# Loading two pairs of the last round in four pieces of 16, 49, 49 and 14 partitions

## The chip, the cores and the metric

The kernel runs on one core of a Trainium2 chip. The metric is the device time of one execution in microseconds, the median over runs.

## What is computed

```python
def reference(x, itok_B_1_198, itok_B_0_7, fside_8xS_0, L0_cond_weights, L1_cond_weights):
    # x (128, 128, 1024) f32; weights (200, 128, 128) and (8, 128, 128); bias (8, 128)
    x = x + einsum('bct,bcd->bdt', x, L0_cond_weights[itok_B_1_198])
    x = x + einsum('bct,bcd->bdt', x, L1_cond_weights[itok_B_0_7]) + fside_8xS_0[itok_B_0_7][:, :, None]
    return x
```

Each of the 128 batches has a matrix x of 128 channels by 1024 steps. It goes through two residual layers, each with a weight chosen by the batch's own index out of a table of 200 or 8. Input and output are 67.1 MB each.

## The kernel before

The two layers are folded into one matrix. With J = I + W1 (the identity plus the chosen second weight) a batch's result is (W0 J + J) applied to x, plus the bias. TensorE makes the product W0 J (`product`, L237, into `m_ps`), VectorE adds J (`sum_m`, L318, into `m_sb`), TensorE applies the sum to x (`results`, L254, into `y_ps`), and the bias is added on the way out of PSUM: the left half of 512 steps by VectorE (`left`, L326), the right half by ScalarE (`right`, L350). Both write back into the buffer from which x was read.

Work goes in pairs of batches. A pair's x is one row of 8 KB in each of 128 partitions, 1 MB. The buffer `xy` is a ring of 8 slots, one pair each; 64 pairs make 8 rounds of 8 slots. The host lays x and out in memory as pairs, so that a load or a store of a pair is one DMA of 128 rows.

The order of the work is written out by hand, engine by engine:

- SyncE's queue issues all loads. For each slot it issues first the two weights W0 of the pair two slots ahead (`load_w0`, L108 to L128, 64 KB each; a weight that an earlier batch has already brought is skipped through the DMA's condition, L113), then waits until the slot's store of the round before has landed (L159), then issues the load of x (`load_x`, L131). The rounds 1 to 6 are a loop (L149), the last round is written out (L156 to L160). The very last pair, slot 7 of the last round, is loaded in four quarters of 512 steps (L165), and two of its four quarters of the result are stored from this queue (L171).
- GpSimd copies each batch's weight and J to the places at which TensorE reads them (`pick`, L188 and L190).
- TensorE runs, for each slot, the first batch of the slot before, the product of this slot, and the second batch of the slot before. It waits for a slot's load (L246), for its summed matrix (L247), and for the PSUM banks to be emptied (L253). Rounds 1 to 7 are one loop (L274), and the last pair stands behind it (L283).
- ScalarE, besides the right halves, issues each pair's store (`store`, L359), and the other two quarters of the last pair (L376).

A DMA adds 16 to its semaphore in all when everything that it moves has landed; a wait for 16 more therefore means that the whole pair is there. Each slot has its own semaphore for loads (`x_loaded[s]`) and for stores (`stored[s]`).

Of the kernel before, what the change touches and what calls it, by code (L numbers as in the profile page):

```python
# [1 line left out]

# [9 lines left out]
def conditioned_residual_kernel(nc, x, cond, w0_t, w1_bias, out):  # L12
# [11 lines left out]
    NP, C, KP, T = x.shape  # L24
    B = NP * KP
    N0, _, D = w0_t.shape
    N1 = w1_bias.shape[1]
    assert C == D == 128
    PAIR = KP
    RING = 8  # L30
    PAIRS = B // PAIR
    ROUNDS = PAIRS // RING
    LAST = RING - 1
# [2 lines left out]
    HALF = T // 2  # L36
    MB = 2
    YB = 2
    assert PAIRS % RING == 0 and HALF <= 512 and RING % MB == 0 and ROUND_B % YB == 0

    x_v = x.rearrange("n c k t -> n c (k t)")
    out_v = out.rearrange("n c k t -> n c (k t)")

    with ExitStack() as ctx:
        def sb(name, shape, dt=F32):
            return ctx.enter_context(nc.sbuf_tensor(name, shape, dt))

        def sem(name):
            return ctx.enter_context(nc.semaphore(name))


        xy = sb("xy", [C, RING, PAIR, T])
# [17 lines left out]
        home_less_b = sb("home_less_b", [B, 1])  # L70
        y_ps = ctx.enter_context(nc.psum_tensor("y_ps", [D, YB, 2, HALF], F32))
        m_ps = ctx.enter_context(nc.psum_tensor("m_ps", [C, MB, 512], F32))
# [12 lines left out]
        x_loaded = [sem(f"x_loaded{s}") for s in range(RING)]  # L85
        w0_loaded = [sem(f"w0_loaded{s}") for s in range(RING)]
        stored = [sem(f"stored{s}") for s in range(RING)]
        last_x_loaded = [sem(f"last_x_loaded{n}") for n in range(2 * PAIR)]
        last_stored = sem("last_stored")
        eye_cleared = sem("eye_cleared")  # L90
# [5 lines left out]
        y_ready = sem("y_ready")  # L96
        left_out = [sem(f"left_out{s}") for s in range(YB)]
        right_out = [sem(f"right_out{s}") for s in range(YB)]

        def half(h):  # L100
            return slice(h * HALF, (h + 1) * HALF)
# [3 lines left out]
        @block.sync  # L105
        def _(sp):
            def words_of(words):
                return nc.values_load_multi_w_load_instructions(  # L108
                    words, engines=(mybir.EngineType.SP,),
                    skip_runtime_bounds_check_because="each word is checked against its own range below")[1]  # L110

            def load_one(b, s, i, needed):
                sp.dma_start(w0_home[:, bass.ds(b, 1), :].rearrange("k b c -> k (b c)"),  # L113
                             w0_t[bass.ds(nc.s_assert_within(i, 0, N0 - 1), 1), :, :].rearrange("n k c -> (n k) c"),  # L114
                             cond=needed).then_inc(w0_loaded[s], 16)

            def load_w0_first(s):
                words = words_of(cond_words[0:1, 0, s * PAIR:(s + 1) * PAIR])
                for k in range(PAIR):
                    load_one(s * PAIR + k, s, words[k], None)  # L120

            def load_w0(r, s):

                sp.wait_ge(w0_loaded[s], r * (PAIR * 16))  # L124
                b = r * ROUND_B + s * PAIR
                words = words_of(load_words[0:1, bass.ds(b, PAIR), :].rearrange("o b f -> o (b f)"))
                for k in range(PAIR):
                    load_one(b + k, s, words[2 * k], nc.s_assert_within(words[2 * k + 1], 0, 1))  # L128

            def load_x(r, s):  # L130
                sp.dma_start(xy[:, s, :, :].rearrange("c k t -> c (k t)"),  # L131
                             x_v[bass.ds(r * RING + s, 1), :, :].rearrange("n c f -> (n c) f"))\
                  .then_inc(x_loaded[s], 16)


            sp.dma_start(j_all[:].rearrange("c n d -> c (n d)"), w1_bias.rearrange("c n d -> c (n d)"))\
              .then_inc(w1_loaded, 16)
            load_x(0, 0)
            sp.wait_ge(cond_loaded, 16)
            for s in range(RING):  # L140
                load_w0_first(s)
                if s < LAST:
                    load_x(0, s + 1)


            sp.wait_ge(home_ready, 4)
            for s in range(LEAD):
                load_w0(1, s)
            with sp.Fori(1, ROUNDS - 1) as r:  # L149
                for s in range(RING):  # L150
                    load_w0(*((r, s + LEAD) if s + LEAD < RING else (r + 1, s + LEAD - RING)))

                    sp.wait_ge(stored[s], r * 16)
                    load_x(r, s)

            for s in range(RING - 1):  # L156
                if s + LEAD < RING:
                    load_w0(ROUNDS - 1, s + LEAD)
                sp.wait_ge(stored[s], (ROUNDS - 1) * 16)  # L159
                load_x(ROUNDS - 1, s)  # L160

            sp.wait_ge(stored[LAST], (ROUNDS - 1) * 16)
            for k in range(PAIR):
                for h in range(2):
                    sp.dma_start(xy[:, LAST, k, half(h)], x[NP - 1, :, k, half(h)])\  # L165
                      .then_inc(last_x_loaded[2 * k + h], 16)
            for k in range(PAIR):

                b = LAST * PAIR + k
                sp.wait_ge(left_out[b % YB], (ROUNDS - 1) * (ROUND_B // YB) + b // YB + 1)  # L170
                sp.dma_start(out[NP - 1, :, k, half(0)], xy[:, LAST, k, half(0)]).then_inc(last_stored, 16)  # L171

            sp.wait_ge(last_stored, 2 * PAIR * 16)
# [51 lines left out]
        @block.tensor  # L225
        def _(pe):
            def product(r, s, first=False):

                pe.wait_ge(picked, r * RING + (s + 1))
                if first:  # L230
                    pe.wait_ge(w0_loaded[s], PAIR * 16)
                if not first or s >= MB:

                    pe.wait_ge(m_ready[s % MB], r * (RING // MB) + s // MB)
                for k in range(PAIR):
                    w0_of_k = w0_home[:, s * PAIR + k, :] if first else w0_pick[:, s, k, :]
                    last = nc.tensor.matmul(m_ps[:, s % MB, k * D:(k + 1) * D], w0_of_k,  # L237
                                            j_pick[:, s, k, 0:D], start=True, stop=True)
                last.then_inc(product_ready, 1)

            def results(r, s, k, first=False, last=False):

                b = s * PAIR + k
                if k == 0:
                    if not last:
                        pe.wait_ge(x_loaded[s], r * 16 + 16)  # L246
                    pe.wait_ge(m_ready[s % MB], r * (RING // MB) + (s // MB + 1))  # L247
                for h in range(2):
                    if last:
                        pe.wait_ge(last_x_loaded[2 * k + h], 16)  # L250
                    if not first or b >= YB:

                        pe.wait_ge((left_out, right_out)[h][b % YB], r * (ROUND_B // YB) + b // YB)  # L253
                    nc.tensor.matmul(y_ps[:, b % YB, h, :], m_sb[:, s, k, :], xy[:, s, k, half(h)],  # L254
                                     start=True, stop=True).then_inc(y_ready, 1)


            pe.wait_ge(ones_ready, 1)
            pe.wait_ge(cond0_row_ready, 1)
            nc.tensor.matmul(cond0_ps[:, 0:B], ones[:], cond0_row[:], start=True, stop=True)  # L260
            nc.tensor.matmul(cond0_ps[:, B:B + 1], cond0_row[:], ones[0:1, 0:1], start=True, stop=True)\  # L261
              .then_inc(cond0_spread, 1)


            product(0, 0, first=True)
            pe.wait_ge(eye_ready, 1)
            pe.wait_ge(home_step, 4)
            nc.tensor.matmul(home_ps[0:1, 0:B], home_less_b[:], eye[:], start=True, stop=True)\  # L268
              .then_inc(home_turned, 1)
            for s in range(1, RING):  # L270
                results(0, s - 1, 0, first=True)
                product(0, s, first=True)
                results(0, s - 1, 1, first=True)
            with pe.Fori(1, ROUNDS) as r:  # L274
                results(r - 1, LAST, 0)
                product(r, 0)
                results(r - 1, LAST, 1)
                for s in range(1, RING):
                    results(r, s - 1, 0)
                    product(r, s)  # L280
                    results(r, s - 1, 1)
            for k in range(PAIR):
                results(ROUNDS - 1, LAST, k, last=True)  # L283

# [120 lines left out]
```

## Time and profile before

| | us |
|---|---|
| median of 3 runs | 352.03 |
| lowest and highest | 350.3 and 352.62 |
| the profiled execution | 353.64 |
| its span in the profile | 351.9 |
| busy in it: TensorE / VectorE / ScalarE / GpSimd | 281.1 / 126.3 / 97.0 / 65.3 |
| moved by DMA | 140.80 MB, mean 400 GB/s |
| granted TensorE clock, mean | 0.93 |

The span is what the profile's rows cover, from the first to the last instruction; the device time lies 1.7 us above it. PE is TensorE, PEld its weight loads, DVE VectorE, ACT ScalarE, POOL GpSimd, SP SyncE; a q behind a name is the engine's own queue of DMA and register instructions. A DMA share of 1.00 means that sixteen DMA engines are busy; where two queues' packets overlap on one engine it goes a little over 1.

### The profile page before, as it was taken

The numbers are of one execution on the slowest core, as the hardware profiler recorded it, in microseconds if no ns is written. First come the engines' busy times: TensorE is split into PE (matmuls) and PEld (weight loads), VectorE is DVE, ScalarE is ACT, GpSimd is POOL, SyncE is SP. The second block draws the span as 40 slices with busy tenths as digits, with TensorE's granted clock in tenths as the row PEclk, the third lists the DMA queues.
The fourth block names the chain that finished last, engine by engine and source line by source line (L and its number), as shares of the span: only waits on it lengthen the run. The fifth ranks groups of instructions, "written<-read, shape, count | busy, mean of one in ns | idle before, by whom it ended". The sixth has DMA issues, their size and how long they took to land.

```text
span 351.9 us, 5351 instructions
## 1 busy us (share of the span) xinstructions
PE 281.1 (80%) x774; PEld 135.6 (39%) x774; DVE 126.3 (36%) x202; ACT 97.0 (28%) x135; POOL 65.3 (19%) x249
## 2 busy tenths in 40 slices
PE   2898499859959977985985996998399678686894
PEld 2454245324424533532532533443155233342341
DVE  3354134404423522441541541444035334342441
ACT  1133035302413321520341331443034212232232
POOL 2400041113113112212212212330131121221200
PEclk9999789969978988998998996999789999999998
DMA  7999999999999999999999999999999999999966
GB/s 282 372 414 422 410 401 413 405 407 403 427 423 424 417 399 419 408 420 386 377 424 415 422 425 422 424 424 420 424 390 401 425 422 415 424 377 415 401 261 247
DMA packets 32554, 140.80 MB, mean 400 GB/s; under 512 B 3617, under 2 KB 15266, under 8 KB 16418
## 3 DMA queue, kind: packets, MB, share of 16 engines
q1 hardware_dynamic: 23184, 74.14, 53.7%
q10 hardware_dynamic: 9362, 66.59, 45.2%
q14 instruction: 7, 0.06, 0.0%
q8 instruction: 1, 0.02, 0.0%
HBM read 76.03 MB, written 67.11 MB: 407 GB/s over the span
## 4 chain that ended last, share of the span: by engine, by line
SPq 44%; DMA 36%; issue 9%; PE 8%; ACT 1%; ACTq 0%
DMA xy<-x 27%; SPq L113 16%; SPq L131 13%; DMA out<-xy 8%; SPq L108 8%; PE y_ps L254 8%; SPq L114 4%; SPq L128 3%; PE m_ps L237 1%; ACT xy L350 1%; DMA cond_words<-cond 0%; SPq L149 0%; ACTq L359 0%; SPq L124 0%; ACTq L358 0%
## 5 line engine op out<-in xcount | busy, mean ns | idle before, releaser
L254 PE MATMUL y_ps<-xy,m_sb 128*128 128x512 f32 x512 | 257.2, 640 | 53.1 <-DMA xy<-x 52.0
L254 PEld LDWEIGHTS y_ps<-xy,m_sb 128*128 128x128 f32 x512 | 96.6, 204 | 162.4 <-issue 130.9
L350 ACT ACTIVATE xy<-y_ps,j_pick 128x512 f32<-128x512 f32 x128 | 88.0, 687 | 236.7 <-PE y_ps L254 236.5
L326 DVE TENSOR_SCALAR xy<-y_ps,j_pick 128x512 f32<-128x512 f32 x128 | 96.1, 751 | 156.3 <-PE y_ps L254 156.3
L188 POOL COPY w_pick<-w_home 128x128 f32 x112 | 32.9, 293 | 258.2 <-issue 258.2
L237 PEld LDWEIGHTS m_ps<-j_pick,w_pick 128*128 128x128 f32 x224 | 37.3, 209 | 30.9 <-issue 30.5
L318 DVE TENSOR_TENSOR m_sb<-m_ps,j_pick 128x256 f32<-128x256 f32 x64 | 27.2, 424 | 57.4 <-PE m_ps L237 54.5
L237 PE MATMUL m_ps<-j_pick,w_pick 128*128 128x128 f32 x224 | 37.0, 291 | 0.0
L190 POOL COPY j_pick<-j_all 128x129 f32 x112 | 33.0, 295 | 0.1
L237 PE MATMUL m_ps<-j_pick,w_home 128*128 128x128 f32 x32 | 6.5, 338 | 10.0 <-issue 6.0
L350 ACT ACT_TABLE_LOAD x7 | 9.0, 1283 | 13.7 <-POOL j_pick L202 7.4
L237 PEld LDWEIGHTS m_ps<-j_pick,w_home 128*128 128x128 f32 x32 | 6.0, 242 | 14.3 <-issue 9.6
L202 POOL COPY j_pick<-j_all 128x129 f32 x16 | 4.7, 295 | 9.9 <-issue 9.5
L260 PE MATMUL cond_ps<-cond_row,ones 1*128 1x128 f32 x2 | 0.8, 482 | 2.4 <-DVE cond_row L289 2.4
L292 DVE TENSOR_TENSOR j_all<-j_all,eye 128x1024 f32<-128x1024 f32 x1 | 1.2, 1225 | 1.9 <-DMA j_all<-w_bias 1.9
L260 PEld LDWEIGHTS cond_ps<-cond_row,ones 1*128 1x128 f32 x2 | 0.5, 306 | 2.4 <-issue 2.4
L309 DVE TENSOR_TENSOR load_words<-home_ps,batch_less_b 1x128 int32<-1x128 f32 x1 | 0.3, 280 | 2.4 <-PE home_ps L268 2.4
L289 DVE CAST cond_row<-cond_words 1x128 f32<-1x128 int32 x1 | 0.2, 215 | 2.1 <-DMA cond_words<-cond 2.1
L268 PE MATMUL home_ps<-eye,home_less_b 128*1 128x128 f32 x2 | 0.6, 394 | 0.0
L261 PEld LDWEIGHTS cond_ps<-ones,cond_row 1*128 1x128 f32 x2 | 0.5, 328 | 0.0
L261 PE MATMUL cond_ps<-ones,cond_row 1*128 1x1 f32 x2 | 0.4, 277 | 0.0
L299 DVE TENSOR_SCALAR same<-cond_ps,cond_col 128x128 f32<-128x128 f32 x1 | 0.4, 351 | 0.0
(16 smaller groups left out, 2.8 us busy)
## 6 DMA issues: line engine op xcount, KB each, us to landing
xy<-x SPq DMA_DIRECT2D x63, 1024.0 KB, 22.0
out<-xy ACTq DMA_DIRECT2D x63, 1024.0 KB, 9.2
w_home<-w_t SPq DMA_DIRECT2D x128, 64.0 KB
xy<-x SPq DMA_DIRECT2D x4, 256.0 KB, 22.8
j_all<-w_bias SPq DMA_DIRECT2D x1, 516.0 KB, 3.4
out<-xy SPq DMA_DIRECT2D x2, 256.0 KB, 4.4
out<-xy ACTq DMA_DIRECT2D x2, 256.0 KB, 4.1
cond_words<-cond ACTq DMA_DIRECT2D x1, 1.0 KB
```

The costliest lines, as they stand in the source:

```text
L108: return nc.values_load_multi_w_load_instructions(words, engines=(mybir.EngineType.SP,), skip_runtime_bounds_check_because="each word is c ...
L113: sp.dma_start(w0_home[:, bass.ds(b, 1), :].rearrange("k b c -> k (b c)"), w0_t[bass.ds(nc.s_assert_within(i, 0, N0 - 1), 1), :, :].rearra ...
L114: w0_t[bass.ds(nc.s_assert_within(i, 0, N0 - 1), 1), :, :].rearrange("n k c -> (n k) c"),
L128: load_one(b + k, s, words[2 * k], nc.s_assert_within(words[2 * k + 1], 0, 1))
L131: sp.dma_start(xy[:, s, :, :].rearrange("c k t -> c (k t)"), x_v[bass.ds(r * RING + s, 1), :, :].rearrange("n c f -> (n c) f"))\
L188: nc.gpsimd.tensor_copy(w0_pick[:, s, k, :], w0_home[:, bass.ds(home, 1), :].rearrange("k b c -> k (b c)"))
L190: last = nc.gpsimd.tensor_copy(j_pick[:, s, k, :], j_all[:, bass.ds(i, 1), :].rearrange("c n d -> c (n d)"))
L237: last = nc.tensor.matmul(m_ps[:, s % MB, k * D:(k + 1) * D], w0_of_k, j_pick[:, s, k, 0:D], start=True, stop=True)
L254: nc.tensor.matmul(y_ps[:, b % YB, h, :], m_sb[:, s, k, :], xy[:, s, k, half(h)], start=True, stop=True).then_inc(y_ready, 1)
L318: nc.vector.tensor_tensor(m_sb[:, s, :, :], m_ps[:, s % MB, 0:PAIR * D].rearrange("c (k d) -> c k d", k=PAIR), j_pick[:, s, :, 0:D], ALU.a ...
L326: nc.vector.tensor_scalar(xy[:, s, k, half(0)], y_ps[:, b % YB, 0, :], j_pick[:, s, k, D:D + 1], None, ALU.add).then_inc(left_out[b % YB], 1)
L350: nc.scalar.activation(xy[:, s, k, half(1)], y_ps[:, b % YB, 1, :], ACT.Identity, bias=j_pick[:, s, k, D:D + 1]).then_inc(right_out[b % YB ...
```

## The change

In the last round the loads of slots 0 and 3 (`FEWER`) are each issued as four DMAs, for partitions 0 to 15, 16 to 64, 65 to 113 and 114 to 127 (`PIECES`), with a semaphore for each of the two slots that gets 16 from every piece. TensorE's loop ends one round earlier and its last round is written out, since in that round slots 0 and 3 wait for 64 on the new semaphore. All other DMAs, the other waits and the arithmetic stay.

```diff
--- before.py
+++ after.py
@@ -1,3 +1,4 @@
+import itertools
 from contextlib import ExitStack
 
 import concourse.bass as bass
@@ -36,6 +37,8 @@
     HALF = T // 2
     MB = 2
     YB = 2
+    FEWER = (0, 3)
+    PIECES = (0, 16, 65, 114, C)
     assert PAIRS % RING == 0 and HALF <= 512 and RING % MB == 0 and ROUND_B % YB == 0
 
     x_v = x.rearrange("n c k t -> n c (k t)")
@@ -85,6 +88,7 @@
         x_loaded = [sem(f"x_loaded{s}") for s in range(RING)]
         w0_loaded = [sem(f"w0_loaded{s}") for s in range(RING)]
         stored = [sem(f"stored{s}") for s in range(RING)]
+        fewer_loaded = [sem(f"fewer_loaded{s}") for s in FEWER]
         last_x_loaded = [sem(f"last_x_loaded{n}") for n in range(2 * PAIR)]
         last_stored = sem("last_stored")
         eye_cleared = sem("eye_cleared")
@@ -157,7 +161,13 @@
                 if s + LEAD < RING:
                     load_w0(ROUNDS - 1, s + LEAD)
                 sp.wait_ge(stored[s], (ROUNDS - 1) * 16)
-                load_x(ROUNDS - 1, s)
+                if s in FEWER:
+                    for a, b in itertools.pairwise(PIECES):
+                        sp.dma_start(xy[a:b, s, :, :].rearrange("c k t -> c (k t)"),
+                                     x_v[(ROUNDS - 1) * RING + s, a:b, :])\
+                          .then_inc(fewer_loaded[FEWER.index(s)], 16)
+                else:
+                    load_x(ROUNDS - 1, s)
 
             sp.wait_ge(stored[LAST], (ROUNDS - 1) * 16)
             for k in range(PAIR):
@@ -238,11 +248,13 @@
                                             j_pick[:, s, k, 0:D], start=True, stop=True)
                 last.then_inc(product_ready, 1)
 
-            def results(r, s, k, first=False, last=False):
+            def results(r, s, k, first=False, last=False, fewer=False):
 
                 b = s * PAIR + k
                 if k == 0:
-                    if not last:
+                    if fewer:
+                        pe.wait_ge(fewer_loaded[FEWER.index(s)], (len(PIECES) - 1) * 16)
+                    elif not last:
                         pe.wait_ge(x_loaded[s], r * 16 + 16)
                     pe.wait_ge(m_ready[s % MB], r * (RING // MB) + (s // MB + 1))
                 for h in range(2):
@@ -271,7 +283,7 @@
                 results(0, s - 1, 0, first=True)
                 product(0, s, first=True)
                 results(0, s - 1, 1, first=True)
-            with pe.Fori(1, ROUNDS) as r:
+            with pe.Fori(1, ROUNDS - 1) as r:
                 results(r - 1, LAST, 0)
                 product(r, 0)
                 results(r - 1, LAST, 1)
@@ -279,6 +291,13 @@
                     results(r, s - 1, 0)
                     product(r, s)
                     results(r, s - 1, 1)
+            results(ROUNDS - 2, LAST, 0)
+            product(ROUNDS - 1, 0)
+            results(ROUNDS - 2, LAST, 1)
+            for s in range(1, RING):
+                results(ROUNDS - 1, s - 1, 0, fewer=s - 1 in FEWER)
+                product(ROUNDS - 1, s)
+                results(ROUNDS - 1, s - 1, 1)
             for k in range(PAIR):
                 results(ROUNDS - 1, LAST, k, last=True)
```

On SyncE's queue, before, in the last round from slot 0 to slot 1 (`w_home<-w_t` is a weight W0, `xy<-x` a load of x with its partitions by elements):

```order
L131 DMA xy<-x 128x2048 [waits stored0]
L108 TENSOR_LOAD load_words [waits w0_loaded3]
L128 ISA x2
L114 ISA x2
L113 ISA
L113 DMA w_home<-w_t 128x128
```

And in the changed kernel at the same place:

```order
L166 DMA xy<-x 16x2048 [waits stored0]
L166 DMA xy<-x 49x2048 x2
L166 DMA xy<-x 14x2048
L112 TENSOR_LOAD load_words [waits w0_loaded3]
L132 ISA x2
L118 ISA x2
L117 ISA
L117 DMA w_home<-w_t 128x128
```

One DMA of 128 rows has become four, ahead of the weights for slot 3; only the first waits for the slot's store. Slot 3 changes in the same way.

On TensorE, in the changed kernel, behind the loop's branch (`m_ps` is a product, `y_ps` a result; the waits of the first slots of the last round):

```order
L286 COMPARE_AND_BRANCH
L266 MATMUL y_ps<-xy,m_sb 128x512 [waits left_out0,m_ready1,x_loaded7]
L266 MATMUL y_ps<-xy,m_sb 128x512 [waits right_out0]
L247 MATMUL m_ps<-j_pick,w_pick 128x128 [waits m_ready0,picked]
L247 MATMUL m_ps<-j_pick,w_pick 128x128
L266 MATMUL y_ps<-xy,m_sb 128x512 [waits left_out1]
L266 MATMUL y_ps<-xy,m_sb 128x512 [waits right_out1]
L266 MATMUL y_ps<-xy,m_sb 128x512 [waits left_out0,m_ready0,fewer_loaded0]
```

Before, behind the branch, only the last pair stood:

```order
L274 COMPARE_AND_BRANCH
L254 MATMUL y_ps<-xy,m_sb 128x512 [waits left_out0,last_x_loaded0,m_ready1]
L254 MATMUL y_ps<-xy,m_sb 128x512 [waits right_out0,last_x_loaded1]
L254 MATMUL y_ps<-xy,m_sb 128x512 [waits left_out1,last_x_loaded2]
L254 MATMUL y_ps<-xy,m_sb 128x512 [waits right_out1,last_x_loaded3]
```

The matmuls of the last round and their order are the same as in the loop; slots 0 and 3 wait for `fewer_loaded0` and `fewer_loaded3` in place of `x_loaded0` and `x_loaded3`.

## Rows read from the trace of the kernel before

**Rows 1.** The page: DMA busy in tenths over 40 slices, and the stores' queue (packets, MB, share of 16 engines).
```profile
DMA  7999999999999999999999999999999999999966
...
q10 hardware_dynamic: 9362, 66.59, 45.2%
```

**Rows 2.** The chain of waits, its end: start us, us, what.
```profile
310.62 3.55 SPq L131
...
314.22 24.60 DMA xy<-x
...
339.05 1.96 PE y_ps L254 x4
...
341.45 5.24 PE y_ps L254 x12
...
346.71 0.69 ACT xy L350
```

**Rows 3.** Windows near the end: from:to, length, busy time by engine, clock, DMA share, GB/s.
```profile
core 0: us, PE busy (x) PEld busy (x) DVE busy (x) ACT busy (x) POOL busy (x), PEclk, DMA share, GB/s
308.00:333.00 25.00, 18.98 (x58) 9.17 (x59) 8.67 (x14) 6.85 (x10) 4.25 (x16) 1.00 1.01 403
333.00:333.50 0.50, 0.50 (x3) 0.26 (x2) 0.21 (x1) 0.02 (x1) 0.38 (x2) 1.00 1.02 430
333.50:334.00 0.50, 0.50 (x3) 0.07 (x1) 0.42 (x1) 0.00 (x0) 0.32 (x2) 1.00 0.47 197
335.00:336.00 1.00, 1.00 (x4) 0.43 (x3) 0.28 (x1) 0.12 (x1) 0.00 (x0) 1.00 0.08 33
343.50:344.50 1.00, 1.00 (x4) 0.50 (x3) 0.44 (x1) 0.39 (x1) 0.00 (x0) 1.00 0.05 20
```

**Rows 4.** Line L131 (loads) from 282 us on: issues, time to landing.
```profile
L131 SPq DMA_DIRECT2D xy<-x x7: 353/703/3552, 282.9 to 314.2; - x7
...
DMA to landing us min/median/max: 23.5/25.7/27.6
```

**Rows 5.** Line L359 (stores) from 282 us on: issues, time to landing.
```profile
L359 ACTq DMA_DIRECT2D out<-xy x12: 338/339/368, 288.2 to 344.0; - x12
...
DMA to landing us min/median/max: 5.0/8.9/10.4
```

**Rows 6.** Waits of TensorE from 308 us on: total us, times, longest.
```profile
PE y_ps L254 <- DMA xy<-x: 6.5, 6, 2.1
```

**Rows 7.** Timeline of TensorE, last round: slots 0 to 6, and slot 7's last wait.
```profile
308.99 1.95 PE L254 MATMUL y_ps<-xy,m_sb 128*128 128x512 f32 x4 [1.01 <-DMA xy<-x]
...
311.23 3.60 PE L254 MATMUL y_ps<-xy,m_sb 128*128 128x512 f32 x8
...
318.20 1.95 PE L254 MATMUL y_ps<-xy,m_sb 128*128 128x512 f32 x4 [1.21 <-DMA xy<-x]
...
324.40 1.98 PE L254 MATMUL y_ps<-xy,m_sb 128*128 128x512 f32 x4 [2.08 <-DMA xy<-x]
...
330.28 1.95 PE L254 MATMUL y_ps<-xy,m_sb 128*128 128x512 f32 x4 [1.73 <-DMA xy<-x]
...
334.56 1.98 PE L254 MATMUL y_ps<-xy,m_sb 128*128 128x512 f32 x4 [0.16 <-DMA xy<-x]
...
339.05 1.96 PE L254 MATMUL y_ps<-xy,m_sb 128*128 128x512 f32 x4 [0.34 <-DMA xy<-x]
...
345.55 0.30 PEld L254 LDWEIGHTS y_ps<-xy,m_sb 128*128 128x128 f32 x2 [0.64 <-DMA xy<-x]
```

**Rows 8.** Timeline of SyncE's queue in the last round: start us, us, issues.
```profile
297.60 0.37 SPq L131 DMA_DIRECT2D xy<-x  x1
299.19 7.27 SPq L113 DMA_DIRECT2D w_home<-w_t  x2
...
310.62 4.60 SPq L131 DMA_DIRECT2D xy<-x  x2
```

## The prediction

> **What bounds the kernel now.** I read the page's table of slices and its DMA queues first. In the slices every digit of the DMA row is 9 up to the last two, which are 6: for 38 slices the sixteen DMA engines together are full. The queue that carries the stores moved 66.59 MB in 45.2% of sixteen engines' span [rows 1]: 0.452 x 16 x 351.9 = 2545 us, or 26.2 GB/s for one engine, so one row of 8 KB (one partition of a pair) takes 8192 / 26.2 = 0.313 us. That is the unit of everything below.
>
> Then the chain of waits, from its end: the load of slot 6 in the last round is issued at 314.22 and lands 24.60 us later, TensorE starts on it at 339.05 and works without a gap through slots 6 and 7 to 346.7, ScalarE adds the bias until 347.4 [rows 2], and the last stores take the remaining 4.5 us of the 351.9. So the end hangs on a load that took 24.6 us. The seven loads of whole pairs in that round took 23.5 to 27.6 us, while the stores of the same stretch, which use the same engines, took 5.0 to 10.4 us [rows 4, 5]: the loads stand in a long queue and the stores do not.
>
> The windows tell how that queue is shaped [rows 3]. Up to 333.5 us all sixteen engines are busy (1.01 and 1.02). In the next half microsecond the share falls to 0.47, and from 335 to 336 it is 0.08, or 0.08 x 16 = 1.3 engines, at 33 GB/s, which is about one engine's 26 and no more. TensorE still waits for slot 6 until 339.05 and at 343.5 to 344.5 the share is 0.05 x 16 = 0.8 engine, 20 GB/s. I read this as **one late engine**: fifteen have finished their part of all loads by about 333.5 to 334, and one goes on alone (beside bursts of stores, which all of them share) for some 11 us more, until the last piece lets TensorE's weight load go at 345.55 [rows 7]. A load counts as landed only when all its shares have, so TensorE runs at the pace of that one engine. In the last round it waits for loads six times, 6.5 us in all [rows 6], longest before slots 3 and 4 (2.08 and 1.73 us) [rows 7].
>
> **The change, part by part.**
>
> *The pieces.* The loads of slots 0 and 3 in the last round keep their bytes (128 rows of 8 KB each), but are cut at partitions 16, 65 and 114. What a cut does depends on how a transfer is dealt out to the engines, and no transfer of another height than 128 is in the trace to show it. I assume equal whole rows for each engine used: 128 rows give sixteen engines 8 rows each, 16 rows give them 1 each, 49 = 7 x 7 goes to seven engines with 7 rows each, 14 to fourteen with 1 each. If small counts always use the first engines, seven engines carry 1 + 7 + 7 + 1 = 16 rows of such a pair, seven more carry 2, and the last two 1. The ends for the late engine are then: it is one of the nine light engines, and loses 6 or 7 rows for each pair, 12 or 14 together, worth 12 x 0.313 = 3.76 or 14 x 0.313 = 4.38 us; or one of the seven heavy ones, and gets 16 rows more, 5.01 us. If pieces were dealt out as evenly as a whole pair is, it would be nothing. I take 13 rows, the middle of the light case: 6.5 rows or 2.03 us from slot 0 on, and **4.07 us** from slot 3 on.
>
> The Trainium skill (DMA: Bandwidth & Descriptors, "Why a DMA increments its semaphore by 16 and not by 1") says that a transfer uses the largest number of engines up to 16 that divides its slowest dimension, and on this path the lowest-numbered ones. By that rule the split is the one assumed here, and the sum stays at 12 or 14 rows; no run shown here tests it. The same page ("Rules for kernel authors") advises whole 128-partition transfers and warns that cutting one up brings nothing: by that advice the time would stay at 352.0, which is the second rival below, and the windows of rows 3 speak against it in this one place, where fifteen of sixteen engines have run dry.
>
> *Does TensorE follow?* It can start a slot when the load has landed and the slot before is done. Slot 0 started at 308.99 after a wait of 1.01; its load comes 2.03 earlier, so only the 1.01 are gained. Slot 1 had no wait of TensorE (3.60 us run on without one) and moves with it. Slot 2 waited 1.21 until 318.20: TensorE would be free at 318.20 - 1.21 - 1.01 = 315.98, the load is there at 318.20 - 2.03 = 316.17, so it starts then, 2.03 early. Slot 3: free at 324.40 - 2.08 - 2.03 = 320.29, landed at 324.40 - 4.07 = 320.33. Slot 4: free at 324.48, landed at 326.21. Slots 5 and 6, with their waits of 0.16 and 0.34, keep the same gap, 4.07 early [rows 7]. So the whole 4.07 reaches the end; the ceiling, had TensorE no wait for a load at all, is 6.5. The stores move with the results, so the late engine has the same rows to serve between two loads as before.
>
> *The heavy engines.* Seven engines get 16 rows more, 16 x 0.313 = 5.01 us. They were through with loads at about 333.5 to 334, so they would be through at about 339. The late engine would be through at about 345.5 - 4.1 = 341.4, still the last by 2.4 us. Cost taken: nothing. The other end: if every one of these rows alternates with a store's row, it takes twice 0.313, 10.0 us in all, to 344.0, which is 2.6 us later than the late engine and leaves 1.5 of the 4.07. I take the low end, since those engines had empty stretches between the bursts of stores (share 0.08 at 335 to 336) in which the rows fit.
>
> *SyncE's queue.* Two issues become eight, so six more. A DMA issue that isn't held up takes 0.37 us there [rows 8], so 6 x 0.37 = 2.2 us. Behind the first group stand the weights of slot 3 and the loads of slots 1 and on, behind the second the weights of slot 5. All of these land more than 20 us after their issue, since they wait behind the late engine's older rows and not for SyncE; 2.2 us are hidden by that. If that cover were gone, they would cost 2.2. The other way, SyncE itself is held up: two weight loads took 7.27 us and two pair loads 4.60 [rows 8], far over 0.37 each, which I read as the late engine's queue having no room. It gets 13 entries fewer, so these stalls should shrink. I take zero for both together.
>
> *TensorE's last round written out.* The loop now runs rounds 1 to 6, and the last round has the same matmuls in the same order with fixed numbers in the waits. One wait differs: slots 0 and 3 wait for all four pieces (64) instead of one load (16). Behind it stand, as before, this slot's matmuls and the next slot's product, which VectorE needs; it ends when the last share lands. Register work disappears beside matmuls of 0.6 us; the new code costs at most a fetch, and TensorE has waits of 1 to 2 us to hide it in. Zero, with 0.3 either way.
>
> **Sum.** 353.64 (profiled execution: span 351.9 and 1.7 around it) - 4.07 = 349.57. The median of the runs before is 352.03, 1.6 below the profiled one, so I forecast 352.03 - 4.07 = 348.0.
>
> **Rivals.**
> (a) *The heavy engines take over as the last.* For it: the share was 1.01 up to 333, so they have no idle time before that. Against: 11 us of lead against 5 of work. Gain 1.5: 350.5.
> (b) *The pieces don't do what they say*, or another wait fills the gap: near-even dealing (1 + 3 or 4 + 3 or 4 + 0 or 1, about 8 rows) leaves the late engine its rows, and the issues are hidden: 352.0.
> (c) *The late engine is one of the seven.* It gets 8 rows more for each pair, 5.01 us with both, and TensorE follows, since each slot from 3 on already waits for it: 352.03 + 5.01 = 357.0, slower. It decides as soon as the late one is among the heavy, whatever else holds. By mere count that is 7 in 16, and no row tells which engine is late; I go well below the count, to 0.13, and the reader should take that as judgement.
> The Trainium skill (same page, "Latency and other measured facts") names engines 7 and 15 as usually slower than the others. Both would be light, with 2 rows and 1; the trace shows that one is late, not which, and by that sentence alone (c) would be left with almost nothing.
>
> **How the numbers follow.** Forecast 0.66, (a) 0.12, (b) 0.09, (c) 0.13. A measurement of this kernel tells about 1% from no change, here 3.5 us, so below 348.5 is faster. The forecast's own range is 346.3 to 349.6: 12 rows alone give 348.3, and the length of the late engine's lead differs from run to run. About four fifths of it, 0.52, lie below 348.5. Same: the rest of it with (a) and (b), 0.14 + 0.12 + 0.09 = 0.35. Slower: 0.13. The range goes from 346.0 to 352.6, the highest of the runs before; (c) and a little at the lower end are left out.
>
> **What would show it.** Right: the windows of the changed kernel's end still show stretches of about one engine, but shorter, some 4 us in place of 11 (the light one ends 4 earlier, the heavy ones up to 5 later); the time from issue to landing of the loads of slots 4 to 6 falls by about 4; TensorE's waits in the last round shrink from 6.5 to about 2.5, with slots 0, 2 and 3 nearly without one; slot 6 starts near 335.0. Heavy engines last (a): waits before slots 5 and 6 grow above 1 us and the share stays near 7/16 before the end. Wrong by (b): waits and landings as before. Wrong by (c): landings of slots 3 to 6 near 30 us and the stretch of one engine at 16 us. Stalls of SyncE longer than 7.27 would mean that the added issues have no cover.

## The result, and the profile after

| | before | changed |
|---|---|---|
| median, us | 351.85 (6 runs, 349.1 to 353.06) | 361.07 (6 runs, 360.37 to 362.25) |
| ratio | | 1.0287, 95% interval 1.0243 to 1.033 |
| the profiled execution, its span | 353.64, 351.9 | 362.05, 360.3 |

The changed kernel is 2.9% slower, 9.2 us. The forecast was 348.0, faster. Medians here and below are over all runs, ratios and their intervals over those runs that lie within 1.5% of the fastest of their kernel, so a ratio and the quotient of two medians can differ by some tenths of a per cent.

The page of the changed kernel, with its DMA row, the rate in each of the 40 slices, and the loads' queue (packets, MB, share):

```profile
DMA  7999999999999999999999999999999999799457
GB/s 269 364 408 419 410 417 420 413 424 423 422 423 424 421 419 420 424 418 417 422 420 422 427 422 428 424 412 413 424 417 423 412 344 361 270 358 415 190 216 262
...
q1 hardware_dynamic: 23240, 74.14, 52.3%
```

Up to the 32nd slice the rate is much as before (behind the first slice 364 to 428 GB/s, before 372 to 427). From there, at 288 us, where the pieces of slot 0 are being moved, it is 344, 361, 270, 358 GB/s; in the stretch from 285 to 330 us it can be set beside the kernel before. Of these four slices only the third shows in the DMA row, with a 7. Windows of the kernel before (columns as in [rows 3]):

```profile
285.00:330.00 45.00, 34.97 (x105) 16.13 (x103) 16.64 (x27) 12.37 (x18) 7.97 (x30) 1.00 1.01 411
```

and of the changed kernel, which answer to [rows 3]:

```profile
285.00:330.00 45.00, 33.39 (x87) 15.85 (x86) 13.96 (x22) 9.62 (x14) 6.37 (x24) 0.85 0.93 348
300.00:315.00 15.00, 7.82 (x19) 3.52 (x18) 3.44 (x6) 2.11 (x4) 1.42 (x6) 0.78 0.80 308
...
338.00:340.00 2.00, 2.00 (x4) 0.80 (x3) 0.73 (x1) 0.00 (x0) 0.77 (x4) 0.50 0.06 25
```

411 - 348 = 63 GB/s less over 45 us are 2.8 MB, which at 411 GB/s take 6.9 us. The last row is the stretch of one engine again: 0.06 x 16 = 1.0 engine, 25 GB/s. It is still there, and now TensorE waits for it for longer. TensorE's waits for loads from 300 us on (answers to [rows 6]) and the timeline around them (to [rows 7]; slots 0, 3 and 4 of the last round):

```profile
PE y_ps L266 <- DMA xy<-x: 12.8, 3, 7.2
```

```profile
312.54 3.78 PE L266 MATMUL y_ps<-xy,m_sb 128*128 128x512 f32 x4 [7.18 <-DMA xy<-x]
...
328.34 1.98 PE L266 MATMUL y_ps<-xy,m_sb 128*128 128x512 f32 x4 [0.92 <-DMA xy<-x]
...
337.15 3.78 PE L266 MATMUL y_ps<-xy,m_sb 128*128 128x512 f32 x4 [4.66 <-DMA xy<-x]
```

Slot 0 starts at 312.54 instead of 308.99, slot 3 at 328.34 instead of 324.40, slot 4 at 337.15 instead of 330.28: 3.6, 3.9 and 6.9 us late. Behind the two long waits four matmul instructions take 3.78 us instead of 1.98, at a granted clock of 0.50, the lower of TensorE's two levels (1.2 GHz). The chain of waits (answers to [rows 2]) ends like this:

```profile
313.48 23.63 DMA xy<-x
...
337.15 3.78 PE y_ps L266 x4
...
349.96 5.17 PE y_ps L266 x12
...
355.15 0.69 ACT xy L369
```

The last load on the chain is now slot 4's. From slot 4 on TensorE has no wait, and needs 355.13 - 337.15 = 17.98 us, where it took 346.69 - 330.28 = 16.41 before. So 6.9 us at slot 4's landing and 1.6 behind it make up, up to rounding, the 8.4 us by which the span grew.

The loads of whole pairs from 282 us on (answers to [rows 4]) take longer from issue to landing:

```profile
L135 SPq DMA_DIRECT2D xy<-x x5: 429/668/3527, 282.7 to 317.3; - x5
...
DMA to landing us min/median/max: 23.6/27.5/34.5
```

SyncE's queue (answers to [rows 8]) is held up more, not less; the last row is the four quarters of slot 7, whose issue took 5.76 us before:

```profile
297.14 6.61 SPq L166 DMA_DIRECT2D xy<-x  x4
305.41 8.03 SPq L117 DMA_DIRECT2D w_home<-w_t  x2
...
317.82 12.97 SPq L175 DMA_DIRECT2D xy<-x  x4
```

Two things can be read off the records directly. First, how a transfer is dealt out: the loads' queue has 23240 packets, 56 more than the 23184 before. The data rows are the same in number, so these are completions, 28 more for each cut pair: 16 + 7 + 7 + 14 = 44 in place of 16. That is what pieces on sixteen, seven, seven and fourteen engines give, as I had assumed. Second, the times at which the sixteen shares of one load completed, from the trace (us, on a clock that runs 11.2 us ahead of the rows in the kernel before and 11.3 in the changed one): slot 4 of the kernel before, and the last seven of the 47 records of slot 0's pieces in the changed kernel.

```
before,  slot 4: 323.2 323.2 323.3 323.5 323.5 323.6 323.7 323.8 323.8 324.9 327.8 328.8 328.8 329.5 329.8 341.3
changed, slot 0: ... 306.7 306.8 307.1 312.7 318.6 322.7 323.8
```

One engine is 11.5 us behind the next: the late engine is real. But four of slot 0's completions are late, one of each piece, so it takes part in both pieces of 49: it is among the seven that carry 16 rows. That is rival (c). Its price was 5 us; the loss is 9.2.

### The profile page after: what moved, and what is told of

Read it like the earlier page. It is cut to its first block, busy times and chain, and to the rows that moved or that the text cites. A ratio compares the mean times of both kernels' runs of the same rounds, so it can differ in the third digit from the quotient of the medians.

```text
span 360.3 us, 5340 instructions
## 1 busy us (share of the span) xinstructions
PE 283.0 (79%) x774; PEld 135.6 (38%) x774; DVE 126.2 (35%) x202; ACT 96.9 (27%) x135; POOL 65.3 (18%) x249
## 3 DMA queue, kind: packets, MB, share of 16 engines
q1 hardware_dynamic: 23240, 74.14, 52.3%
## 4 chain that ended last, share of the span: by engine, by line
SPq 44%; DMA 33%; PE 12%; issue 9%; ACT 1%; ACTq 0%
DMA xy<-x 25%; SPq L117 17%; SPq L135 12%; PE y_ps L266 11%; DMA out<-xy 8%; SPq L112 6%; SPq L118 4%; SPq L132 3%; SPq L166 2%; PE m_ps L247 1%; ACT xy L369 1%; DMA cond_words<-cond 0%; SPq L153 0%; ACTq L378 0%; ACTq L377 0%
```

## The experiments

The theory at first was (c): the late engine has 16 rows more, and what is missing from 9.2 comes from TensorE's lower clock and from waits. Rivals: the additional issues and the wait for four pieces; the written-out code. Of each kernel its edit to the changed kernel is shown; ratios are to the kernel before on the same chip.

**1. Even pieces**

```diff
-    PIECES = (0, 16, 65, 114, C)
+    PIECES = (0, 32, 64, 96, C)
```

> The changed kernel with the four pieces of 32 partitions each: as many DMAs and the same wait for four, but every engine carries its 8 rows. Theory (the late engine is among the seven that carry 16 rows): the rows are gone, so the time is that of the kernel before, 352 within 1%. Rival 1 (six more issues on SyncE, or waiting for four pieces, cost the 9.2 us): it stays near 361. Rival 2 (both share it): about 356.

Measured 356.0 against 351.0, ratio 1.0155 (1.0082 to 1.0228). Neither the theory nor rival 1: with no row moved to any engine about half of the loss stays. It is rival 2's number, with nothing yet to explain it.

**2. Only the last round written out**

```diff
-    FEWER = (0, 3)
+    FEWER = ()
```

> Only TensorE's last round is written out, every pair is loaded whole. Theory: 352 within 1%, TensorE's waits in the last round as before (6.5 us). Rival (code that has to be fetched, or another pace of TensorE): above 355.

350.4 against 351.0, ratio 0.9978 (0.994 to 1.0017). The code costs nothing measurable.

**3. and 4. One slot alone**

```diff
-    FEWER = (0, 3)
+    FEWER = (0,)
```

and in experiment 4 `FEWER = (3,)`.

> Only slot 0 of the last round in the pieces 16, 49, 49, 14. Theory: the late engine gets 8 rows more instead of 16, 8 x 0.313 = 2.5 us, and TensorE's one long wait before slot 0 costs some of its clock: 354 to 357, half of the loss. Rival (the loss comes with slot 3, near the end, alone): 352.

> Only slot 3 of the last round in the pieces 16, 49, 49, 14. [...] Rival (the whole loss of the changed kernel is slot 0's, since it was 6.9 of 9.2 alone): 351 to 353.

Slot 0 alone: 357.9 against 351.0, ratio 1.0213 (1.0178 to 1.0247), more than expected. Slot 3 alone: 355.3 against 350.2, ratio 1.0114 (1.0026 to 1.0201), above the 351 to 353 of its rival. Each of the two costs by itself. By the medians they cost 6.9 and 5.1, more in sum than the 9.2 of both; but slot 3's interval reaches from 0.9 to 7.0 us, so this difference isn't shown. In the profile of slot 0 alone the loads of slots 5 and 6 land 2.6 and 3.2 us later than in the kernel before, near the 2.5 of eight rows, but slot 4's lands 2.3 earlier, and the span is 4.6 longer: a plain shift by eight rows it is not.

**5. and 6. Which engine is late**

```diff
-    PIECES = (0, 16, 65, 114, C)
+    PIECES = (0, 96, 113, C)
```

and in experiment 6, with a cut of its own for each slot,

```diff
-    PIECES = (0, 16, 65, 114, C)
+    PIECES = {0: (0, 112, 117, 121, 124, 126, 127, C), 3: (0, 112, 119, 125, C)}
...
```

> Pieces of 96, 17 and 15 partitions. If a transfer uses the largest number of engines up to 16 that divides its rows, and always the first ones, the first engine carries 6 + 17 + 1 = 24 rows of such a pair, the last 6, all others 7. Theory A (the late engine is the first): 32 rows more for it, 10 us and more of loss, 362 to 370, and the last of the 16 completions of the pieces stands far behind the others. Theory B (the late engine is another of the seven): it loses 2 rows, and the first engine, 10 us heavier, only just catches up with it: 350 to 354.

> To count which engine is late. Slot 0 in pieces of 112, 5, 4, 3, 2, 1 and 1 partitions, slot 3 in 112, 7, 6 and 3, so that an engine takes part in more or fewer of them by its number, if a transfer of 7 rows or less uses the first ones with one row each. Of the completions of slot 0's pieces the late engine's stand far behind the rest: 5 of them if it is the second engine, 4 the third, 3 the fourth, 2 the fifth, 1 the sixth or seventh; of slot 3's, 2 would be the seventh and 3 the fifth or sixth. If the late engine were the first, it would be 7 and 4. Time about 352 to 357: the late engine gets at most 4 rows more.

Experiment 5: 355.1 against 351.0, ratio 1.0163 (1.0096 to 1.023), far from the 362 of theory A and above theory B, as the even pieces are. In its loads two engines stand behind the rest (the last three completions of slot 4: 322.2, 338.5 and 341.5): the first one with its 32 rows more, and another, so the late one isn't the first. Experiment 6, one run: 356.5. Its last completions of the two cut loads:

```
slot 0: ... 304.3 304.5 304.7 305.2 307.0 319.1 320.1
slot 3: ... 325.2 325.3 325.3 327.3 338.0 338.9 339.9
```

Two late ones of slot 0's pieces, three of slot 3's. By the counts laid down in the expectation two would be the fifth engine, and three the fifth or sixth: it is the fifth.

**7. and 8. Four engines or five**

```diff
-    PIECES = (0, 16, 65, 114, C)
+    PIECES = (0, 60, C)
```

and in experiment 8 `PIECES = (0, 85, 113, C)`.

> Slots 0 and 3 in two pieces of 60 and 68 partitions: by the division rule 60 rows go to fifteen engines, 4 each, and 68 = 4 x 17 to the first four, so these carry 21 rows, the fifth to fifteenth 4. Theory (the late engine is the fifth): it loses 8 rows, 2.5 us, while the first four get 26 more, 8.1 us, and end at about 333.5 + 8.1 = 341.6, still ahead of it: 348 to 352. Rival (it is one of the first four): 8 us and more later, above 359.

> Slots 0 and 3 in pieces of 85, 28 and 15: 85 = 5 x 17 goes to the first five engines, so each of these carries 17 + 2 + 1 = 20 rows of a pair. Theory (the late engine is the fifth): 24 rows more for it, 7.5 us, and TensorE at its lower clock after the long waits: 359 to 364. Rival (the late engine is the sixth or seventh): it loses 10 rows and the time is 349 to 354.

Four: 355.9 against 350.8, ratio 1.0167 (1.0111 to 1.0224). Five: 363.7 against 350.8, ratio 1.0334 (1.0285 to 1.0382). So with 20 rows instead of 4 of each cut pair on the fifth engine the time is 7.8 us longer, and in the two profiles slot 4's load lands at 341.69 instead of 330.86 us, 10.8 later, where 32 rows at 0.313 are 10.0: the late engine's rows are on the path. (The second kernel also has one piece more for each pair; that alone was not priced.) Relieving the engine by eight rows did not bring the forecast 2.5. One reason stands in the completions of slot 4: five, not one, are behind the rest (329.4, 339.2, 340.2, 341.4 and 342.3 on the completions' clock, the other eleven by 322.5), so the four engines with 26 rows more had come as far back as the late one. The even pieces, which load no engine more, cost 5.0 us all the same: the cut has a cost beside the rows.

**9. and 10. TensorE kept busy through its waits**

```diff
+            def keep_busy(n):
+                for _ in range(n):
+                    nc.tensor.matmul(cond0_ps[:, :], eye[:], w0_home[:, 0:4, :].rearrange("k b c -> k (b c)"),
+                                     start=True, stop=True)
...
             for s in range(1, RING):
+                keep_busy({1: 7, 5: 5}.get(s, 0))
```

and in experiment 10 `{5: 3}`. The results go to a bank of PSUM that nothing reads any more.

> The changed kernel, with matmuls of no use put ahead of TensorE's long waits in the last round: 7 before slot 0, 5 before slot 4, 0.9 us each, so that they fill waits of 7.2 and 4.7 us. The loads are as in the changed kernel. Theory (5 us of the 9.2 come from the rows, about 2 to 4 from TensorE at its lower clock of 1.2 GHz after the waits): the granted clock stays at 1.00 behind slots 0 and 4, the four pairs after slot 4's landing take 16.0 us instead of 18.0, and the time is 357 to 359.5. Rival (the clock is not on the path, the loads alone set the end): 361.

> As the changed kernel, with only three matmuls of no use, 2.7 us, before slot 4 of the last round, where TensorE waited 4.7 us and then ran 18.0 us to its end, the first part at 1.2 GHz. Unlike 7 and 5 of them they cannot outlast the wait. Theory (the lower clock behind this wait is on the path): the granted clock stays 1.00 behind slot 4, the stretch from slot 4 to TensorE's end is 15.1 to 16.5 us, the time 358 to 359.5. Rival (the clock costs nothing there): 361.

363.2 against 350.2, ratio 1.0338 (1.0266 to 1.0411), and 362.1 against 350.8, ratio 1.0282 (1.0224 to 1.034). Neither is faster than the changed kernel. In experiment 9:

```profile
336.92 4.46 PE L296 MATMUL cond_ps<-w_home,eye 128*128 128x512 f32 x10
341.21 1.88 PE L266 MATMUL y_ps<-xy,m_sb 128*128 128x512 f32 x4
...
351.13 5.32 PE L266 MATMUL y_ps<-xy,m_sb 128*128 128x512 f32 x12
```

The clock does stay up behind slot 4: 351.13 + 5.32 - 341.21 = 15.2 us, against 17.98. But the matmuls of no use outlast the load, which by its completions had landed at 337.8, by 3.4 us and give all of it back. Experiment 10's three ran from 339.56 to 342.30, behind another long wait (6.02 us, before slot 3), with the clock at 0.50 there. They too outlast the load, which had landed at 339.9, though they were meant not to; the clock is 1.00 behind them, and from slot 4 to TensorE's end it takes 15.2 us, as the theory said, but the start is 2.2 us late. So neither run has the clock up without a delay, and what the clock takes on net is not measured. An estimate from the changed kernel's own rows: its load of slot 5 had landed at 342.40; with the clock up from 337.15 on, TensorE would be done with slot 4 at 341.0, wait for that landing, and need another 11.4 us by experiment 9's rows, to 353.8 instead of 355.1. That is 1.3 us of the 9.2.

**11. Halves: one cut, no rows moved**

```diff
-    PIECES = (0, 16, 65, 114, C)
+    PIECES = (0, 64, C)
```

> Slots 0 and 3 in two pieces of 64 partitions, every engine with its 8 rows. It prices the cut without any shift of rows, beside the four pieces of 32, which came out 0.8 to 2.2% slower than the kernel before. Theory (the cut has a cost of its own for each issue, which I had put at zero): 0.3 to 1% above the kernel before, 351.5 to 354. Rival (those four pieces only met slow neighbours in the queue by chance): the same as before within 0.3%.

356.0 against 350.8, ratio 1.0118 (1.0077 to 1.016): two additional DMAs in 350 us cost 5.2 by the medians, 4.1 by the ratio. Theory and rival both miss. That isn't 0.37 us an issue. Its windows (the profiled execution is a long one of its kind, 359.1):

```profile
285.00:330.00 45.00, 32.00 (x89) 14.54 (x87) 14.62 (x23) 10.43 (x16) 6.37 (x24) 0.95 1.02 361
```

Here is the row that gives it away: **the share is 1.02 and the rate is 361 instead of 411**. All engines are busy and move 12% less; 50 GB/s over 45 us are 2.3 MB or 5.5 us. In the packets the rows of the loads started in that stretch take 0.416 us on the mean, against 0.326 in the kernel before. Each engine still has its 8 rows, but not at the same time as before: a half of 64 partitions gives the sixteen engines four rows each, and all of these are in the same half of the memory. In the changed kernel the same stretch has both kinds of loss: the share falls from 1.01 to 0.93, which is 3.6 us of the 45 with engines idle, and that leaves about 3.3 of its 6.9 to rows that take longer.

**12. and 13. The same number of DMAs, cut along the row**

```diff
-    PIECES = (0, 16, 65, 114, C)
+    PIECES = (0, T, 2 * T)
...
-                        sp.dma_start(xy[a:b, s, :, :].rearrange("c k t -> c (k t)"),
-                                     x_v[(ROUNDS - 1) * RING + s, a:b, :])\
+                        sp.dma_start(xy[:, s, :, :].rearrange("c k t -> c (k t)")[:, a:b],
+                                     x_v[(ROUNDS - 1) * RING + s, :, a:b])\
```

and in experiment 13 `PIECES = (0, HALF, T, T + HALF, 2 * T)`.

> Slots 0 and 3 in two DMAs again, but cut along the row: 128 partitions by 1024 elements each, so every engine fills the same partitions as with a whole pair. It stands against the two pieces of 64 partitions (1.2% slower than before). Theory P (the cut by partitions costs because it makes several engines write to the same partitions' ports at once): as the kernel before, 349.5 to 352.5. Rival I (the additional issue and completion cost it): about 355 as with 64 and 64.

> Four DMAs of 128 partitions by 512 elements for slots 0 and 3, as many DMAs and the same wait for four as in the changed kernel. Theory P: as the kernel before within 0.5%. Rival I: as with four pieces of 32 partitions, 354 to 358.

351.6 against 351.1, ratio 1.0019 (0.9974 to 1.0065), and 351.9, ratio 1.0026 (0.9993 to 1.0059). As many DMAs and issues as with two or four pieces by partitions, the same waits, and no loss. Windows of experiment 12:

```profile
285.00:330.00 45.00, 36.49 (x96) 17.22 (x95) 15.41 (x24) 10.78 (x16) 8.50 (x32) 0.87 1.01 408
```

408 GB/s again at the same share. The rival of issues and waits falls; the direction of the cut decides. The rate of one such stretch is no exact price, though: experiment 13's profile has 392 GB/s there and experiment 16's 390, at a share of 1.00 each, and neither kernel loses time.

**14. Each cut alone**

```diff
             sp.wait_ge(last_stored, 2 * PAIR * 16)
...
+            x0 = xy[:, 0, :, :].rearrange("c k t -> c (k t)")
+            sp.dma_start(x0, x_v[0, :, :]).then_inc(probe[0], 16)
+            sp.wait_ge(probe[0], 16)
+            for a, b in ((0, 64), (64, 128)):
+                sp.dma_start(x0[a:b, :], x_v[0, a:b, :]).then_inc(probe[1], 16)
+            sp.wait_ge(probe[1], 2 * 16)
...
```

> All pairs whole (TensorE's last round written out). Behind the kernel's last store SyncE loads one pair seven times, each alone and waited for: whole; 64 + 64; 4 x 32; 16, 49, 49, 14; two and four columns pieces of 128 partitions; 60 and 68. Theory P: whole 8 x 0.313 + about 2 = 4.5 to 5 us; 64 + 64 and 4 x 32 half as fast in the transfer, 7 to 7.5 us, though no engine has more than 8 rows; columns as the whole one; the changed kernel's cut 7 to 9; 60 and 68 about 8.6 (21 rows on four engines). Rival I: 64 + 64 and 4 x 32 like the columns, all within 0.7 us of the whole pair.

The output is written before these loads begin, and each cut is measured once. Windows from one first issue to the next: whole; 64 + 64; 4 x 32; 16, 49, 49, 14; two pieces along the row; four along the row; 60 and 68 (the last window ends near the landing).

```profile
349.72:354.49 4.77, 0.00 (x0) 0.00 (x0) 0.00 (x0) 0.00 (x0) 0.00 (x0) 0.50 0.60 220
354.49:361.47 6.98, 0.00 (x0) 0.00 (x0) 0.00 (x0) 0.00 (x0) 0.00 (x0) 0.50 0.64 150
361.47:368.31 6.84, 0.00 (x0) 0.00 (x0) 0.00 (x0) 0.00 (x0) 0.00 (x0) 0.50 0.70 153
368.31:376.72 8.41, 0.00 (x0) 0.00 (x0) 0.00 (x0) 0.00 (x0) 0.00 (x0) 0.50 0.37 125
376.72:381.95 5.23, 0.00 (x0) 0.00 (x0) 0.00 (x0) 0.00 (x0) 0.00 (x0) 0.50 0.58 201
381.95:387.77 5.82, 0.00 (x0) 0.00 (x0) 0.00 (x0) 0.00 (x0) 0.00 (x0) 0.50 0.57 180
387.77:398.50 10.73, 0.00 (x0) 0.00 (x0) 0.00 (x0) 0.00 (x0) 0.00 (x0) 0.50 0.35 98
```

With no other traffic a whole pair takes 4.77 us, halves 2.2 us more, quarters by partitions 2.1 more, the changed kernel's cut 3.6 more; two pieces along the row 0.5 more, four 1.1. Theory P's numbers come close, but for 60 and 68 (10.7 instead of 8.6) and for these small costs along the row. In the trace's packets a row of 8 KB takes 0.309 us in the whole load by the median and 0.358 on the mean, and 0.590 and 0.553 in the halves: the engines are slowed in their work, not left without it. The changed kernel's cut is another case: its rows take 0.316 by the median and 0.390 on the mean, hardly more than in the whole load, and the share is 0.37. There seven engines work through 16 rows each, 8 more than in a whole pair, which is 8 x 0.309 = 2.5 of its 3.6 us. The Trainium skill (SBUF — State Buffer, "Door 1: The DMA port swizzle") says that partitions reach the memory through sixteen ports, and that partitions 0 to 63 use only eight of them, as do 64 to 127. The runs agree: halves move at 150 GB/s against 220, fixed time included, and with the two engines of a port taking turns 0.309 would become 0.618, an estimate beside the median of 0.590. What the runs show is the slowing and the direction of the cut; that the ports are its reason is argued. A cut by partitions also cuts the source in memory into blocks of its own, which a cut along the row does not, and no run tells the two apart.

**15. Four slots in halves**

```diff
-    FEWER = (0, 3)
-    PIECES = (0, 16, 65, 114, C)
+    FEWER = (0, 1, 3, 4)
+    PIECES = (0, 64, C)
```

> Pieces of 64 and 64 partitions for four slots (0, 1, 3, 4) instead of two. Theory P (each such load holds the engines 2.2 to 2.4 us longer, as measured alone, and the DMA engines are the bound): twice the loss of two slots, 2 to 3.2%, 358 to 362. Rival (the loss comes from one event, such as TensorE's clock): as with two slots, 1.2%, about 355.

359.4 against 350.1, ratio 1.0222 (1.0151 to 1.0293), and 340 GB/s from 285 to 330 us. Twice the slots, about twice the loss (9.3 us by the medians, 7.8 by the ratio): the cost adds up by slot, 1.9 to 2.3 us each here, 2.2 alone.

**16. A wait for each batch**

```diff
+                if fewer:
+                    pe.wait_ge(fewer_loaded[FEWER.index(s)][k], 16)
                 if k == 0:
-                    if fewer:
-                        pe.wait_ge(fewer_loaded[FEWER.index(s)], (len(PIECES) - 1) * 16)
-                    elif not last:
+                    if not last and not fewer:
...
```

(with slots 0 to 6 cut along the row into the two batches, a semaphore for each)

> Meant to beat both: every pair of the last round but the last is loaded in two DMAs of 128 partitions by 1024 elements, one for each batch, with a semaphore each, and TensorE waits for a batch instead of a pair. The cut along the row cost nothing measurable; the first batch is there up to half a load earlier, 4 rows or 1.3 us on the late engine, more where stores' rows alternate. Expected: 348.5 to 351, if the end hangs on the arrival of slot 4's or 6's first batch. Rival (TensorE waits for the second batch instead, since the late engine sets both): within 0.3% of the kernel before.

350.8 against 350.1, ratio 1.0009 (0.9982 to 1.0037). The rival: no gain. From 300 us on TensorE has more and shorter waits, eight of 8.5 us in all and none above 1.5, where the kernel before has seven of 9.2 with a longest of 2.7. That fits the rival's reason, that the second batch still arrives with the late engine; it was not looked at further. No kernel of this study is measurably faster than the one before.

## Why the prediction was wrong

*The late engine.* Right, and shown by the completions: one engine, 11.5 us behind the next, sets when loads land. The reading of the 0.08 share as one engine held. (The DMA row of the page has a 7 in its first slice, so the engines are full in 37 slices and not in 38; nothing rests on it.)

*The dealing of the pieces.* Right: 28 completions more for a cut pair, as 16, 7, 7 and 14 engines give.

*The heavy engines at nothing.* Right: in the changed kernel fifteen engines completed their shares of slot 6 within 2.7 us of each other, and the late one 17.6 us behind them.

*"I take 13 rows, the middle of the light case."* Wrong in sign, and the first step that failed. The late engine is the fifth and carries 16 rows of a cut pair, 16 more in all, 5.0 us by the row's price, where I had taken 13 fewer, 4.07 us. I had put 7 in 16 by count and went down to 0.13, leaning on the sentence of the Trainium skill (DMA: Bandwidth & Descriptors, "Latency and other measured facts") that names engines 7 and 15. The Trainium skill puts this, in the same place, to DMAs whose descriptors software writes; the queues here stand as hardware_dynamic in [rows 1], so it did not bear on this kernel, and neither of its engines is the late one. No row of the trace named the engine, so the count should have stood: 7 in 16 for the slower side, too much to leave (c) outside the range. What the late engine's rows cost is seen between experiments 7 and 8: 7.8 us for 32 rows. The signs given for (c) came: the longest landing of a whole pair is 34.5 us, TensorE follows slot 4's landing, 6.9 us late, and SyncE stalls for more than 7.27.

*"The loads ... keep their bytes", with a price of 0.313 us for each row wherever it goes.* Wrong, and the term that no rival held. The cut by partitions alone, with no row moved between engines, costs 2 to 2.6 us for each pair (experiments 11, 14, 15), and a row takes 0.590 us in such a load, not 0.309. In the changed kernel's own form less of this is seen: loaded alone it takes 3.6 us more, of which 2.5 are the 8 rows more on each heavy engine. In the profile its slot 4 lands 6.9 us late, of which 5.0 are, by the price, the late engine's 16 rows, and 1.9 are left for the cut and for all else; TensorE's slower stretch adds 1.6. This is an account of one execution and an estimate. How much of the 9.2 belongs to each can't be given exactly: a kernel in which the late engine carries more rows and the rows keep their pace was not tried.

*SyncE's six issues at nothing.* The issues themselves cost nothing measurable, as said: experiment 13 has as many. But "these stalls should shrink" failed: four quarters took 12.97 us to issue instead of 5.76, and two weights 8.03 instead of 7.27. From 300 to 315 us, with SyncE in such a stall, the DMA share was 0.80, and the loads' queue started 183 packets of 2 KB or more where the kernel before started 331. That the stalls come from the late engine's queue, which got longer instead of shorter, fits this but was not tested.

*TensorE written out*, at zero: right within the noise, ratio 0.9978 (0.994 to 1.0017).

*The rules on whole transfers.* I set aside the advice to load 128 partitions whole because fifteen of the sixteen engines have run dry near the end. But that is true only behind 333.5 us. The cut loads were issued at 278.0 and 297.1 us and had landed by 312.5 and 328.3, and there the engines were full (share 1.01 before). A reason to expect a loss and not merely no gain is the port map of the Trainium skill (SBUF — State Buffer, "Door 1: The DMA port swizzle"), which I had not weighed; the first rival to write down for a cut along partitions was that one.

*The range.* 346.0 to 352.6 left out (c) alone, and (c) at 357.0 was itself short by 4, so no range made from my rivals would have held 361.1.

## What to carry to other kernels

Cut a DMA along the row, not along the partitions: at equal bytes and issues, the one cost nothing measurable in this kernel (0.5 to 1.1 us for a pair loaded alone) and the other about 2 us a megabyte. A DMA share of 1.0 doesn't say that the engines work at their pace; read the GB/s beside it, and compare the two between kernels, but let the times decide, since two kernels here moved 5% less in the same stretch and lost nothing. Where one engine of sixteen is late, find out which before moving work: small pieces of 1 to 7 rows and a count of the late completions told it in one run.

## What was not expected of the hardware

Rows of 8 KB took 0.309 us in a whole load and 0.590 in loads of 64 partitions on the same sixteen engines (medians, each load measured once). The late engine is the fifth of sixteen by experiment 6, and experiments 5, 7 and 8 agree with it; it was 11.5 us behind the next one at slot 4 of the kernel before, and 17.2 at slot 4 of the changed kernel. What makes it late was not looked for. And inside the kernel the additional DMAs themselves cost nothing measurable where they were cut along the row, even eight in place of two.
